# A first LoRA product in float32 from a small load, with the first set's matmuls and splits in another order

## The reference, cut to what matters

```
h  = relu(x @ wi.T + 2 * (x @ A_c.T) @ B_c.T + 2 * (x @ A_e.T) @ B_e.T)      # e: the sequence's expert
c  = h @ wo.T + 2 * (h @ A'_c.T) @ B'_c.T + 2 * (h @ A'_e.T) @ B'_e.T        # D = 256, F = 1024, ranks 16
p  = softmax(mean_t(c) @ gate_w); two largest of 8, their shares scaled to a sum of 1
out = x + sum over the two: share * (gelu(c @ w1[e] + b1[e]) @ w2[e] + b2[e])
```

## Time and profile before

| | |
|---|---|
| median of 3 runs | 273.61 us (273.35 to 273.63) |
| profiled execution: its time | 273.51 us |
| profiled execution: its span, first to last instruction | 271.3 us |
| TensorE matmul busy | 265.5 us (98% of the span) |
| VectorE, ScalarE, GpSimd busy | 159.7, 168.8, 143.7 us |
| DMA | 18.99 MB, mean 70 GB/s |

### The profile page before, as it was taken

One profiled execution on the slowest core, in us unless ns is written; L12 is line 12 of the kernel. 1 busy time (PEld: TensorE's weight loads), 2 busy tenths in 40 slices (PEclk: granted clock), 3 DMA queues, 4 the chain that ended last, 5 costly groups with the idle time before them and its releaser, 6 DMA issues.

```text
span 271.3 us, 3608 instructions
## 1 busy us (share of the span) xinstructions
PE 265.5 (98%) x1172; PEld 214.5 (79%) x1172; DVE 159.7 (59%) x269; ACT 168.8 (62%) x272; POOL 143.7 (53%) x171
## 2 busy tenths in 40 slices
PE   8999999999999999999999899999999999999995
PEld 3588888888888887878888688888788888888883
DVE  1754436243389635656594776666955667665654
ACT  2645453364635458987986877776766776775650
POOL 0074342553746677689619998566366366431100
PEclk9999999999999999999999999999999999999999
DMA  6996220201024022112201122112022015000004
GB/s 181 282 308 164 93 77 0 81 1 39 4 60 128 7 80 78 40 37 79 70 10 33 46 80 77 35 42 80 5 74 77 18 62 189 4 2 1 0 0 155
DMA packets 17169, 18.99 MB, mean 70 GB/s; under 512 B 1984, under 2 KB 14528, under 8 KB 17152
## 3 DMA queue, kind: packets, MB, share of 16 engines
q1 hardware_dynamic: 16304, 17.60, 21.4%
q10 hardware_dynamic: 848, 1.18, 1.4%
HBM read 16.67 MB, written 2.10 MB: 69 GB/s over the span
## 4 chain that ended last, share of the span: by engine, by line
PE 90%; ACT 3%; DMA 2%; POOL 2%; DVE 1%; issue 1%; SPq 1%; DVEq 0%; ACTq 0%
PE out_ps L642 15%; PE out_ps L643 15%; PE out_ps L646 15%; PE hid_ps L642 14%; PE hid_ps L643 14%; PE hid_ps L646 14%; DMA lora_raw<-in_lora 2%; ACT up_hi L488 1%; POOL up_lo L383 1%; ACT hid_ps L520 1%; PE hid_ps L749 1%; PE hid_ps L762 1%; SPq L281 1%; DVE hid_lo L889 1%; ACT hid_hi L534 0%
## 5 line engine op out<-in xcount | busy, mean ns | idle before, releaser
L383 POOL TENSOR_TENSOR up_lo<-up_raw,up_hi 128x512 fp32r<-128x512 f32 x39 | 50.4, 1311 | 49.0 <-ACT up_hi L488 49.0
L642 PE MATMUL out_ps<-hid_hi,down_hi 128*128 128x512 f32 x192 | 74.9, 390 | 0.0
L643 PE MATMUL out_ps<-hid_lo,down_hi 128*128 128x512 f32 x192 | 74.7, 389 | 0.0
L646 PE MATMUL out_ps<-hid_hi,down_lo 128*128 128x512 f32 x192 | 74.7, 389 | 0.0
L642 PE MATMUL hid_ps<-act_hi,up_hi 128*128 128x512 f32 x176 | 69.2, 393 | 0.9 <-DVE hid_lo L889 0.9
L643 PE MATMUL hid_ps<-act_lo,up_hi 128*128 128x512 f32 x176 | 68.7, 390 | 0.0
L646 PE MATMUL hid_ps<-act_hi,up_lo 128*128 128x512 f32 x176 | 68.5, 389 | 0.0
L520 ACT ACTIVATE hid_ps<-hid_ps,bias_sb 128x512 f32<-128x512 f32 x64 | 41.6, 662 | 39.8 <-DVE hid_ps L913 30.4
L889 DVE SCALAR_TENSOR_TENSOR hid_lo<-hid_ps,mix,hid_hi 128x512 fp32r<-128x512 f32 x64 | 47.7, 745 | 25.4 <-ACT hid_hi L534 24.9
L389 POOL TENSOR_TENSOR down_lo<-down_raw,down_hi 128x512 fp32r<-128x512 f32 x24 | 31.6, 1317 | 45.0 <-ACT down_hi L498 44.8
L534 ACT ACTIVATE hid_hi<-hid_ps,mix 128x512 fp32r<-128x512 f32 x64 | 42.3, 690 | 1.7
(11 more groups left out here) (75 smaller groups left out, 201.9 us busy)
## 6 DMA issues: line engine op xcount, KB each, us to landing
up_raw<-in_w SPq DMA_DIRECT2D x16, 256.0 KB, 3.1
down_raw<-in_w SPq DMA_DIRECT2D x16, 256.0 KB, 2.6
down_raw<-in_woT SPq DMA_DIRECT2D x8, 256.0 KB, 3.7
lora_raw<-in_lora SPq DMA_DIRECT2D x10, 192.0 KB, 7.1
up_raw<-in_wiT SPq DMA_DIRECT2D x7, 256.0 KB, 5.5
outT<-x_sb SPq DMA_DIRECT2D x6, 256.0 KB, 3.2
x_sb<-in_xT SPq DMA_DIRECT2D x1, 1024.0 KB, 10.4
x_sb<-in_xT ACTq DMA_DIRECT2D x2, 256.0 KB, 4.7
```

Source lines behind the costliest of these rows:

```text
L383: ins = eng.tensor_tensor(up_lo[:, n, cols], up_raw[:, n, cols], f32(up_hi[:, n, cols]), ALU.subtract)
L642: eng.matmul(out, w_h, a_h, start=start, stop=False, skip_group_check=onto)
L643: eng.matmul(out, w_h, a_l, start=False, stop=False, skip_group_check=onto)
L646: return eng.matmul(out, w_l, a_h, start=False, stop=stop, skip_group_check=onto)
```

## The change

1. A load of 64 KB, one copy (32 rows) of lot 0, goes first in SP's queue into a tile `lora_first`; lot 0 itself (192 KB) goes behind x0b. The product for set 0's up weights takes `lora_first` as it is, in float32, without split. Lot 0 is split later: set 1 and the following need it.
2. ScalarE copies lot 0 after `up0_high`, VectorE takes its low part after `up0_low`.
3. `x0_low` of channel block 1 (two of the four) goes from VectorE to GpSimd, ahead of the low parts of lot 1; the semaphore is now one for each block.
4. Set 0's tiles run in pairs of one token half (`first_pair`): for block 0 high x high of two tiles, then high x low of two, the same for block 1, then the four low x high. Each waits only for its own operand. `down_factor(0)` stands behind both pairs, `up_factor(1)` between them.
5. The matmuls on zeros are 12 and 3 instead of 22 and 6.

The diff, cut to its core:

```diff
-    WARM_UP = 22
-    WARM_MORE = 6
+    WARM_UP = 12
+    WARM_MORE = 3
...
+        def x0_low(eng, kd, t):
+            eng.wait_ge(s_x0hi, kd + 1 if t == 0 else KD + 1)
+            eng.tensor_tensor(act_lo[:, 0, kd * NT + t, :], x_sb[:, kd, half(0, t)],
+                              f32(act_hi[:, 0, kd * NT + t, :]), ALU.subtract).then_inc(s_x0lo[kd], 1)
...
-            load_lora(0, 0, e)
+            eng.dma_start(lora_first[:, :], lora[bass.ds(e, 1), 0:G, 0:LOT].rearrange("e r c -> (e r) c"))\
+               .then_inc(s_lora_first, 16)
             eng.dma_start(x_sb[:, :, half(0, 1)], xT[:, half(0, 1)].rearrange("(k p) t -> p k t", p=P))\
                .then_inc(s_x0b, 16)
+            load_lora(0, 0, e)
             load_lora(0, 2, e)
...
-            after((s_rank, 1))
+            x0_low(eng, 1, 0)
+            x0_low(eng, 1, 1)
+            after((s_x0lo[1], NT))
             lora_low(0, 1)
             up_low(1)
             down_low(0)
...
             x0_high(0)
-            lora_high(0, 0)
             x0_high(1)
             up0_high(0)
             up0_high(1)
+            lora_high(0, 0)
             lora_high(0, 2)
...
+            def first_pair(t):
+                for kd in range(KD):
+                    eng.wait_ge(s_x0hi, kd + 1 if t == 0 else KD + 1)
+                    eng.wait_ge(s_up0hi, kd + 1)
+                    for f in range(2):
+                        w = up_hi[:, 0, block(kd * 2 + f)]
+                        eng.matmul(hid_ps[:, 2 * t + f, :], w, act_hi[:, 0, kd * NT + t, :], start=(kd == 0), stop=False)
+                    eng.wait_ge(s_x0lo[kd], t + 1)
+                    for f in range(2):
+                        w = up_hi[:, 0, block(kd * 2 + f)]
+                        eng.matmul(hid_ps[:, 2 * t + f, :], w, act_lo[:, 0, kd * NT + t, :], start=False, stop=False)
+                for f in range(2):
+                    for kd in range(KD):
+                        eng.wait_ge(s_up0lo, kd + 1)
+                        ins = eng.matmul(hid_ps[:, 2 * t + f, :], up_lo[:, 0, block(kd * 2 + f)],
+                                         act_hi[:, 0, kd * NT + t, :], start=False, stop=(kd == KD - 1))
+                    ins.then_inc(s_up, 1)
...
+            def first_up_factor(*outs):
+                eng.wait_ge(s_lora_first, 16)
+                for kd in range(KD):
+                    eng.matmul(outs[kd], lora_first[:, block(kd)], lora_first[:, SW:2 * SW], start=True, stop=True)\
+                       .then_inc(s_prod0, 1)
...
             warm_up(WARM_UP)
-            up_factor(0, out_ps[:, 0, 0:SW], out_ps[:, 1, 0:SW])
+            first_up_factor(out_ps[:, 0, 0:SW], out_ps[:, 1, 0:SW])
             warm_up(WARM_MORE)
-            plain_tile(0, 0)
-            plain_tile(0, 1)
+            first_pair(0)
             up_factor(1, out_ps[:, 2, 0:SW], out_ps[:, 2, SW:2 * SW])
-            plain_tile(0, 2)
-            plain_tile(0, 3)
+            first_pair(1)
+            down_factor(0, out_ps[:, 3, :])
...
-            x0_low(0, 0)
-            lora_low(0, 0)
-            x0_low(1, 0)
+            x0_low(eng, 0, 0)
             merge0(0)
             merge0(1)
             up0_low(0)
             up0_low(1)
+            lora_low(0, 0)
             lora_low(0, 2)
-            x0_low(0, 1)
-            x0_low(1, 1)
+            x0_low(eng, 0, 1)
```

## The result

The change made the kernel slower: 275.34 us median of 11 executions (274.45 to 278.47), against 273.61 (273.35 to 273.85). The ratio is 1.0073, with a 95% interval of 1.005 to 1.0096. The forecast was 273.7, its range 272.8 to 274.6.

The account below looks back on a forecast made before the run. TensorE was taken as the bound, a string of matmuls behind the head, with GpSimd's chain ending last in set 1. +0.25 - 0.12 = +0.13 us on 273.51 gave 273.64, median 273.7, range 272.8 to 274.6.

Parts of the forecast that it names:

- The head: Before set 0: float32 product takes 0.9 us, first pair starts near 7.75, 2.6 us earlier than 10.35.
- The landings: SP's queue behind x0b: with 64 KB more ahead, lot 0 lands at 10.03 and lot 2 at 10.75.
- the bounds of 12.1 to 12.9: Behind set 0's first pair: TensorE restarts at 12.5 after 1.9 us of nothing, within these limits.
- the loss of +0.25 at the third matmul: Set 1's first tile: third matmul waits for GpSimd's up_low(1), at 17.15 where it stood at 16.90.
- GpSimd's chain ends last: Sets 0 and 1: GpSimd's x, lot 1 and up weights 1 end last, at 17.05; chance 0.61.
- The small gap at the product for set 2: At 20.67, before set 2: the 0.12 us wait for GpSimd's lot 3 goes, giving back 0.12 us.
- Fewer matmuls on zeros cost nothing by themselves: they filled waiting time: Before the first product: 12 and 3 matmuls on zeros instead of 22 and 6 cost nothing.
- The clock's fall: Rival: clock falls in the stop behind the first pair, third matmul at 18.2, +1.05, 274.7 us; chance 0.16.
- GpSimd not last: Rival, set 1: GpSimd's chain meets TensorE's own 16.3 to 16.5, giving 272.8 to 273.1 us; chance 0.18.
- the full head start: Rival: work starts 2.6 us earlier and lots are there in time, giving 270.9 us; chance 0.03.

Follow-up runs that it names:

- x on VectorE: Changed kernel with the two low parts of x block 1 back on VectorE: median 274.29 us, ratio 1.0023 to the kernel before.
- lots first: Changed kernel with only the load order altered, lots 0 and 2 ahead of the second half of x: median 274.03 us, 273.7 in executions not fallen.

## Why the prediction was wrong

Two steps failed: the landings of lots 0 and 2, put 0.6 and 0.7 us too early, and the matmuls on zeros, whose removal was put at nothing. The path that ends last was right.

**The head: right.** The factors landed at 6.5 (5.9), the float32 product took 1.06 us from start to the next matmul (0.9), real work began at 8.38 (7.75). That this is worth nothing while the lots are late held: zeros 22 and 6 put it off to 9.75 at no cost.

**The landings: the term that was mis-sized.** "Lot 0 lands at 10.03 ... lot 2 10.75" came from 64 KB more ahead at the speed between two landings. In the changed kernel they landed at 10.6 and 11.4:

```profile
x_sb<-in_xT SPq DMA_DIRECT2D x1, 512.0 KB, 6.7
lora_raw<-in_lora SPq DMA_DIRECT2D x1, 192.0 KB, 7.0
lora_raw<-in_lora SPq DMA_DIRECT2D x1, 192.0 KB, 7.2
```

The 512 KB took the same 6.7 us as in the earlier trace rows, with 128 KB less ahead of them, and each lot behind them took 0.8. TensorE restarted at 13.13, outside the bounds of 12.1 to 12.9. So the loss of +0.25 at the third matmul became +1.05 (17.95 against 16.90), 0.7 of the 0.8 more by the landings and 0.1 by GpSimd (1.80 against 1.70).

The order of loads did it: that edit alone took 1.3 us off. With it and x on VectorE lot 2 landed at 8.3, and the same 960 KB were all there 1.2 us sooner. What doesn't hold is counting the bytes ahead. When the 960 KB (0.98 MB) were there, at 11.44, SP's queue had moved 1.62 MB in the changed kernel's trace: the transfers behind them had moved at the same time. With the lots first and x on VectorE it was 1.45 MB at 10.26. The traffic differs too, 240 GB/s of the core from 8 to 10 us in the changed kernel and 309 in the other. Why the order changes either isn't shown.

**GpSimd's chain ends last: right.** Moving x back to VectorE took 0.7 us off, and 0.6 in the version with lots first. The small gap at the product for set 2 went, as forecast, but that gave nothing back: behind its wait the third matmul took 0.33 us to the next one and not 0.23, and the product for set 2 stands 1.06 us later than before.

**"Fewer matmuls on zeros cost nothing by themselves: they filled waiting time": wrong.** The clock's fall had a chance of 0.16 as a rival, and it was priced as something that happens to all executions or to none. It happened in 7 of 17, at about 1.2 us each by the medians (276.19 against 275.0). That the zeros matter is shown: none of six fell with 22 and 6 back, and all six of the kernel before fell with 12 and 3. Which stand lets it fall is not. The one in the head goes with it (13 of 36 with the lots first and 12 and 3 zeros, 0 of 24 with 16 and 4), but loosely: in one profile with 16 and 4 TensorE stood 0.8 there, and none of those twelve fell. The one behind the first pair may do it too (4 of 12 with the zeros up to the first product, 0 of 6 with both filled). The trace of before held a warning: its 22 zeros covered the time to the first product almost whole.

**GpSimd not last, and the full head start:** neither came about. The second was nearer than its 0.03: with the lots first TensorE did run through from 8.85 to 15.4, and it needed only lots at 9, which that order gives (7.3 and 8.3).

In sum, in the profiled execution, which didn't fall: +0.13 forecast; +1.05 measured at the third matmul, +1.06 at the product for set 2 and +1.22 at the last matmul, and the time 1.27 longer. At 69 us TensorE is 0.98 later than before; the rest came in behind that and wasn't followed. The median of all executions that didn't fall lies 0.2 above the profiled one, and the falls lift the median of all by another 0.3, to 275.34.

## What to carry to other kernels

An early start of the engine that bounds a kernel is worth what the next needed transfer allows: when a load is put behind another, follow who waits for it, and try the order of loads by itself, since here it was worth 1.2 to 1.3 us at equal bytes. The bytes ahead in a queue didn't give the landing here, since what stood behind moved too. Dummy matmuls in a wait help to hold the clock, and they should come out only with the wait; judge that by many executions, since one profile may show none of it. A subtraction moved to an idle engine comes out even only if it doesn't run beside one of the same kind.

## What the runs showed of the hardware

- Stands of TensorE go with a fall of the clock, and mostly in some executions only. The stands given here are those of each kernel's profiled execution, and only one of these had fallen (to 1.2 GHz, with 3.2 us before the first product; all six of that kernel fell). With 1.6 us behind the first pair 4 of 12 fell; with 1.1 us there and 0.6 in the head none of nine; with 0.4 to 0.6 in the head 5, 4 and 4 of 12. So the length of a stand alone doesn't tell, and what else does is open. The rise after the start varied too, from about 4.2 to past 5.9 us. It is read from the distance of the matmuls on zeros (0.43, then 0.21), since the column of the granted clock reads 1.00 there all the time. The Trainium skill (TensorE: Matmul & The Clock Gate, What's actually happening) lets the clock follow recent activity, and the falls agree with it.
- Subtractions of two SBUF operands on VectorE and GpSimd held each other up, and the one that started first ran at its own speed: 0.69 and 1.80 us when VectorE was 0.04 ahead, 1.28 and 1.67 when GpSimd was 0.16 ahead. The Trainium skill (GPSIMD Engine Reference, Key points) names this contention for two SBUF inputs, and both profiles agree with it. In the second it was VectorE that was held up, and with the lots first alone again (1.73).
- A float32 product of 32 rows, two of 256 columns, took 1.13 us, 1.06 from its start to the next matmul, and shows as four matmuls; two of 256 columns and 96 rows in the rounded type took 0.40 to 0.51, and 0.24 to 0.34 to the next.
